# A diffusion block's cross attention: the context loaded with its inner dimensions exchanged and normalised in that form

## The reference

```python
q_c = _ln(x) @ W_qc + b_qc
kv_c = _ln(context) @ W_kvc + b_kvc          # context: 32 x 128 tokens x 128 channels
k_c, v_c = jnp.split(kv_c, 2, axis=-1)
...                                          # 16 heads of 8 channels
c_attn_w = jax.nn.softmax(jnp.einsum('bhqd,bhsd->bhqs', q_c, k_c) * scale, axis=-1)
c_attn_out = jnp.einsum('bhqs,bhsd->bhqd', c_attn_w, v_c)
...
x = x + c_attn_out @ W_cproj + b_cproj
```

## Time and profile before

| | |
|---|---|
| runs shown | median 561.09 us of 3 (560.26 to 562.99) |
| the profiled execution | 563.06 us, its span 561.2 us |
| granted TensorE clock, mean | 0.99 of full speed |
| setup, up to about | 30 us |
| attention rounds | about 30 to 300 us, 35 us a round |
| MLP and second layer | the rest |

### The profile page before, as it was taken

The page is one execution under the profiler, slowest core; times in us unless marked ns, Lnnn a source line. Parts: engine busy times, 40 slices in busy tenths (PEclk is TensorE's granted clock), DMA queues, the critical chain, the costliest instruction groups (busy, mean ns, idle before and its releaser), DMA issues.

```text
span 561.2 us, 16447 instructions
## 1 busy us (share of the span) xinstructions
PE 529.0 (94%) x6175; PEld 384.4 (68%) x6177; DVE 433.5 (77%) x1271; ACT 380.5 (68%) x889; POOL 276.2 (49%) x296
## 2 busy tenths in 40 slices
PE   6988999999999999999999989998999999999995
PEld 5745666666566665666676756665788788888885
DVE  4778889788989889888887667767586786786565
ACT  6537778587787886878787685555754864864862
POOL 5637849569498686888860413224124124124100
PEclk9989999899999999999999999999999999999998
DMA  4665635634254343543330001001011011010000
GB/s 133 153 181 137 179 100 151 139 94 106 61 137 120 79 125 81 132 117 100 82 79 4 2 23 36 1 20 37 3 39 56 23 35 56 23 38 14 20 20 19
DMA packets 52939, 41.47 MB, mean 74 GB/s; under 512 B 6369, under 2 KB 52226, under 8 KB 52866
## 3 DMA queue, kind: packets, MB, share of 16 engines
q1 hardware_dynamic: 50792, 36.72, 24.9%
q10 hardware_dynamic: 2074, 3.77, 2.4%
HBM read 12.16 MB, written 2.10 MB: 25 GB/s over the span
## 4 chain that ended last, share of the span: by engine, by line
PE 63%; DVE 15%; POOL 7%; DMA 5%; issue 4%; ACT 4%; SPq 2%; ACTq 0%; DVEq 0%; POOLq 0%
PE PS L958 31%; PE PS L1833 7%; PE PS L1799 5%; PE PS L1885 4%; DVE NM L1613 3%; PE PS L1897 3%; PE PS L994 2%; DMA Qs<-MT 2%; PE PS L1817 2%; PE PS L1855 2%; PE PS L1890 2%; SPq L1343 2%; DVE r_T L933 2%; DVE r_R L936 1%; PE PS L1877 1%
## 5 line engine op out<-in xcount | busy, mean ns | idle before, releaser
L1613 DVE TENSOR_REDUCE NM<-PS 128x4 f32<-128x512 f32 x256 | 163.3, 681 | 30.0 <-PE PS L1799 29.4
L1499 ACT ACTIVATE PR<-PS 128x512 f32<-128x512 f32 x256 | 139.7, 600 | 27.0 <-PE PS L1817 26.4
L1799 PEld LDWEIGHTS PS<-Ks,Qs 64*128 64x128 bf16 x1024 | 57.3, 94 | 53.8 <-DVE NM L1613 28.7
L1799 PE MATMUL PS<-Ks,Qs 64*128 64x128 bf16 x1024 | 83.4, 218 | 5.6 <-DVE NM L1613 3.8
L1817 PE MATMUL PS<-Qs,Ks 64*128 64x128 bf16 x1024 | 83.6, 218 | 3.9 <-DMA Qs<-MT 3.3
L1833 PE MATMUL PS<-PR,Va 128*32 128x128 f32 x2048 | 83.3, 281 | 0.0
L744 ACT ACTIVATE r_HID<-PS,ANC 128x128 f32<-128x128 f32 x224 | 62.4, 378 | 18.5 <-PE PS L958 18.5
L655 POOL TENSOR_TENSOR m_veps<-m_mv,m_eps 128x4 f32<-128x4 f32 x16 | 3.6, 225 | 129.7 <-DVE m_mv L820 129.7
L1833 PEld LDWEIGHTS PS<-PR,Va 128*32 128x32 f32 x2048 | 48.5, 110 | 20.2 <-ACT PR L1499 6.9
L1817 PEld LDWEIGHTS PS<-Qs,Ks 64*128 64x128 bf16 x1024 | 57.1, 94 | 7.5 <-DMA Qs<-MT 3.8
L958 PE MATMUL PS<-r_NXS,r_WNS 128*128 128x512 f32 x168 | 52.6, 421 | 0.0
(11 more groups left out here) (198 smaller groups left out, 1110.1 us busy)
## 6 DMA issues: line engine op xcount, KB each, us to landing
Qs<-Qp SPq DMA_DIRECT2D x96, 128.0 KB
Ks<-Kp SPq DMA_DIRECT2D x90, 128.0 KB
CTXG<-in_ctx SPq DMA_DIRECT2D x8, 256.0 KB, 3.9
r_CTX<-in_ctx SPq DMA_DIRECT2D x8, 256.0 KB, 2.9
r_CTXT<-in_ctxt SPq DMA_DIRECT2D x8, 256.0 KB, 3.3
out<-X SPq DMA_DIRECT2D x8, 256.0 KB, 2.3
X<-in_x SPq DMA_DIRECT2D x7, 256.0 KB, 4.5
W<-in_weights ACTq DMA_DIRECT2D x2, 855.0 KB
```

The costliest lines, as they stand in the source:

```text
L1499: nc.scalar.activation(PR[:, u, :], T_BANK[u % 2][:, :], ACT.Exp, scale=SCALE)\
L1613: nc.vector.tensor_reduce(out=NM[:, c.b // 2, c.second, u // 2, u % 2 * 4:u % 2 * 4 + 4, 0], in_=S_BANK[score_bank(c, u)[0]][:, :].rearran ...
L1799: last = nc.tensor.matmul(S_BANK[bank][:, j * P:(j + 1) * P], Qs[c.stack][rows, lo + j, cols], Ks[c.stack][rows, lo + j, cols], start=True ...
```

## The change

The context is also read from `in_ctxt`, an input that holds it with channels ahead of tokens (the second layer read it before already). A group now takes this way: `CTXG` is loaded and its statistics taken as before. Then three steps on SP, given by `spread_steps`: "rows store" waits for `rstd` and writes means and deviations, 512 numbers of 4 bytes each, to a scratch tensor `rows` in DRAM by two DMAs; "rows turned" loads the exchanged context to `XN[2]` or `XT[2]`, channels on partitions; "rows load" waits for the two stores and reads each row of 512 numbers back to all 128 partitions, the means over `CTXG`, the deviations to a new tile `ROWS`. POOL's norm then waits for these three loads and works in place on the exchanged tile; PE's `k` and `v` products read it. PE's transposes `xt_c` and ACT's copies are gone. The load of the next group's `CTXG` waits for the norm, as before.

```diff
+def spread_steps(t0, t1, t2, g):
+    return [(t0, "rows", "store", g, 0), (t1, "rows", "load", g, 0), (t2, "rows", "turned", g, 0)]
...
@@ regular_steps(i)
-            + stats_steps(19.2, 20.2, "ln_c", i) + norm_steps(23.0, "ln_c", i)
+            + stats_steps(19.2, 20.2, "ln_c", i) + spread_steps(26.0 if i == NG - 4 else 28.0, 29.0, 28.5, i) + norm_steps(29.5, "ln_c", i)
...
-            + fill_steps(14.0, "xt_c", i - 1, (1, 14.1))
...
@@ crossed_steps(i)
-    return (load_steps(1.0, g + 1) + stats_steps(5.2, 6.2, "ln_c", g + 1) + norm_steps(7.0, "ln_c", g + 1)
+    return (load_steps(1.0, g + 1) + stats_steps(4.9, 5.9, "ln_c", g + 1)
+            + spread_steps(8.05, 10.7, 9.0, g + 1) + norm_steps(14.1, "ln_c", g + 1)
...
-            + load_steps(12.0, g + 2) + stats_steps(21.2, 22.2, "ln_c", g + 2) + norm_steps(23.0, "ln_c", g + 2)
-            + fill_steps(0.2, "xt_c", g, (1, 0.3)) + fill_steps(2.0, "k0", i + 1, (0, 2.1), (1, 2.2))
+            + load_steps(12.0, g + 2) + stats_steps(19.2, 20.2, "ln_c", g + 2)
+            + spread_steps(22.0, 24.6, 25.1, g + 2) + norm_steps(27.0, "ln_c", g + 2)
+            + fill_steps(2.0, "k0", i + 1, (0, 2.1), (1, 2.2))
...
-            + fill_steps(16.0, "xt_c", g + 1, (1, 16.1)) + fill_steps(18.0, "k1", i + 1, (0, 18.1), (1, 18.2))
+            + fill_steps(18.0, "k1", i + 1, (0, 18.1), (1, 18.2))
...
+        rows = nc.dram_tensor("rows", [2, GB, P], F32).ap()
...
+        ROWS = sb("ROWS", [P, GT])
...
+        def context_turned(g):
+
+            return (XN[2], XT[2])[g % 2]
...
@@ SP
+                elif ev[:2] == ("rows", "store"):
+                    g = ev[2]
+                    sp.wait_ge(ln_rstd[2], g + 1)
+                    sp.dma_start(rows[0].rearrange("b p -> p b"), mv[:, 2, :, 0],
+                                 allow_slow_non_contiguous=True).then_inc(rows_stored, 16)
+                    sp.dma_start(rows[1].rearrange("b p -> p b"), rstd[:, 2, :],
+                                 allow_slow_non_contiguous=True).then_inc(rows_stored, 16)
+                elif ev[:2] == ("rows", "load"):
+                    g = ev[2]
+                    sp.wait_ge(rows_stored, 32 * (g + 1))
+                    for k, to in enumerate((CTXG[:, :, :].rearrange("p b h -> p (b h)"), ROWS[:, :])):
+                        row = rows[k:k + 1].rearrange("k b p -> k (b p)")
+                        sp.dma_start(to, row.to_broadcast([P, GT])).then_inc(rows_loaded, 16)
+                elif ev[:2] == ("rows", "turned"):
+                    g = ev[2]
+                    if g > 1:
+                        sp.wait_ge(*last_of_context(g - 2))
+                    sp.dma_start(context_turned(g)[:, :].rearrange("h (b p) -> h b p", b=GB),
+                                 ctxtin[bass.ds(g * GB, GB)].rearrange("b h p -> h b p")).then_inc(rows_loaded, 16)
...
@@ POOL
+                elif ev[:2] == ("norm", "ln_c"):
+                    if ev[3] == 0:
+                        g, turned = ev[2], context_turned(ev[2])[:, :]
+                        pool.wait_ge(rows_loaded, 48 * (g + 1))
+                        nc.gpsimd.tensor_tensor(turned, turned, CTXG[:, :, :].rearrange("p b h -> p (b h)"),
+                                                ALU.subtract).then_inc(ln_centred[2], 1)
+                        pool.wait_ge(ln_centred[2], g + 1)
+                        nc.gpsimd.tensor_tensor(turned, turned, ROWS[:, :], ALU.mult).then_inc(ln_done[2], 1)
...
@@ PE
+                        if name[0] == "k" and kind == CROSS:
+                            pe.wait_ge(ln_done[2], content(int(name[1]), g)[1] + 1)
```

More of the change, by code:

```diff
@@ L1193, in build_block @@
         ctx_loaded = sem("ctx_loaded")
+        rows_stored = sem("rows_stored")
+        rows_loaded = sem("rows_loaded")
         score_done = sem("score_done")
@@ L1241, in build_block @@
         OgT = [sb(f"OgT{k}", [P, GT]) for k in range(2)]
-        LN_KIND = {"ln_s": 0, "ln_x": 1, "ln_c": 2, "xt_s": 0, "xt_x": 1, "xt_c": 2}
+        ROWS = sb("ROWS", [P, GT])
+        LN_KIND = {"ln_s": 0, "ln_x": 1, "ln_c": 2, "xt_s": 0, "xt_x": 1}
         WEIGHT = {"q": ("q", "qc"), "k": ("k", "kc"), "v": ("v", "vc")}
@@ L1252, in turn_target @@
                 return XT[1]
-            return XT[0] if name == "xt_s" or isinstance(g, int) and g in (4, 6) else XT[2]
+            return XT[0]
         def source(name, it):
@@ L1259, in source, with last_of_context @@
                 return XT[mem]
-            return XT[1] if name[0] == "q" else XT[2 * mem]
+            return XT[1] if name[0] == "q" else context_turned(content(mem, it)[1])
+        def context_turned(g):
+            return (XN[2], XT[2])[g % 2]
+        def last_of_context(g):
+            mem = 0 if (CROSS, g) in HOLDS[0] else 1
+            return bank_filled[f"v{mem}"], HOLDS[mem].index((CROSS, g)) + 1
         def pair_of(c):
@@ L1397, in body @@
                     nc.gpsimd.memset(Ks[2][:, :, :].bitcast(F32), 0.0).then_inc(stack_init, 1)
+                elif ev[:2] == ("norm", "ln_c"):
[6 more added lines that the diff above has]
+                        nc.gpsimd.tensor_tensor(turned, turned, ROWS[:, :], ALU.mult).then_inc(ln_done[2], 1)
                 elif name == "norm" and not (ev[1] == "ln_x" and ev[2] in OF_DVE) and not (ev[1] == "ln_s" and ev[2] < 2):
                     g, k = ev[2], LN_KIND[ev[1]]
-                    x = CTXG[:, :, :] if k == 2 else X[:, bass.ds(g * GT, GT)].rearrange("p (b h) -> p b h", b=GB)
+                    x = X[:, bass.ds(g * GT, GT)].rearrange("p (b h) -> p b h", b=GB)
                     to = XN[k][:, :].rearrange("p (b h) -> p b h", b=GB)
@@ L1541, in body @@
                         last.then_inc(bank_read[name], 1)
-                elif name == "read" and ev[1] in ("xt_x", "xt_c"):
+                elif name == "read" and ev[1] == "xt_x":
                     name, g = ev[1:3]
@@ L1872, in body @@
                         return
-                    if name in ("xt_s", "xt_x", "xt_c"):
+                    if name in ("xt_s", "xt_x"):
                         k = LN_KIND[name]
```

4 lines of the change are left out of this document (2 added, 2 removed).

## The result

The changed kernel takes 662.31 us (median of 4 runs, 660.08 to 664.06) against 562.04 us for the kernel before beside it: ratio 1.177, 95% interval 1.171 to 1.182. The forecast was 576.0. The sign was right; the loss is 100 us where 15 were worked out. The profiled execution took 661.73 us, its span 659.8 us.

What follows compares the result with a forecast made beforehand. PE, 94% busy, paces the rounds, but delays of POOL or SP ahead of step 18 show almost in full. 4.3 + 2.9 + 3.7 + 2.0 + 2.0 = 14.9 us on 563.06 gives 578.0, or 576.0 as median; range 562.5 to 585.

Steps and rivals of the forecast that it cites:

- I take 2.3, since the bytes are few, and keep 3.9 as the bound.: Time in us from a store's issue to its landing in DRAM: 2.3 from `out`, bound 3.9 from the context's load.
- The third rival: Slow stores: landing 3.9 us or more instead of 2.3, total 585 and beyond with slower ones; chance 0.10.
- While SP waits for the stores to land, nothing urgent stands behind it: SP in C0 to C3: the row maxima of step 3 come some 9 us after those of step 27.
- The path that I wrote down for the regular rounds: C0 to C3: norm 1.0 to 1.75 us late, delaying `rstd`, splits, SP's moves and PE at step 18; +4.3 us.
- Row loads and norm: Per group: row loads land in 3.3 us, second issued 0.6 later; POOL's norm takes 2.2; whole chain 9.0 us.
- The crossed rounds, 2.9 + 3.7 + 2.0 + 2.0 = 10.6 us: Losses at C4 (end of round 4), round 5 up to step 18, second half of round 5, and round 6.
- The mechanism for C4's `k0`: Step 2 of round 5: PE waits in order for POOL's late norm of C4, about 3 us; term +2.9.
- where I charged 4.3: C0 to C3: norm ends 5.3 us too late in sum, less 1.0 PE may have had to spare.
- the first rival: Way through DRAM hidden in C0 to C3, only later rounds pay, 10.6 us at most: about 570; chance 0.22.
- What was to be seen: Profile signs: late norm of C0 to C3, PE's waits, SP waiting for `rows`, 32 fewer transposes.
- PE's waits for Q or K at step 18 of most rounds: PE should wait there for Q or K, longest in round 5, some 5 us.
- the stores' wait on SP is far from 2.3 us: One of three stated signs of being wrong: SP's wait for the stores' landing, taken as 2.3 us.

Runs made afterwards that it cites:

- the wide version: Changed kernel with mean and deviation in one store of 128 pieces of 32 bytes and one 512 KB row load per group: 598.4 us, ratio 1.060.

## Why the prediction was wrong

The direction and its reason, that PE's saved work counts for little and the way through DRAM for much, were right. The sum was wrong, by these steps.

1. **"I take 2.3, since the bytes are few, and keep 3.9 as the bound."** This step failed. The landing is 9.7 to 11.4 us after the second store's issue in the four regular rounds. The row of `out` was the wrong neighbour: its pieces are 512 bytes and this store's price is in its pieces. The bound was no bound either: it was the row of a load, and not even the slowest of 256 KB, since the page has 4.5 us for `X<-in_x`. The third rival had the cause, slow stores, at chance 0.10, but carried it only to 585 "and beyond", as a landing that is waited for.
2. **"While SP waits for the stores to land, nothing urgent stands behind it."** With a landing of 2.3 us that held; with 10.7 SP's wait pushed the row maxima of step 3 out by 6.8 us. And what I had not in the sum at all is that the stores delay what does not wait for them: 656 of 662 us in the version whose stores nobody reads, up to 51 us where they are added to the kernel before. The path that I wrote down for the regular rounds, norm too late, then splits, then SP's moves, did hold, with an overrun of 11.1 us for C2 where I had 1.0. But PE meets it first at the row maxima of step 11, which SP issues behind those moves; the waits for row maxima come to 40.2 us, those for K and Q to 2.6 and 1.9.
3. **Row loads and norm.** I took 3.3 us and 2.2 us. The loads land 4.3 to 6.5 us after the second one's issue in the regular rounds, and 8.1 for C5, so this term too was 30% to 100% too small there; the norm takes 180.25 to 182.86, 2.6.
4. **The crossed rounds, 2.9 + 3.7 + 2.0 + 2.0 = 10.6 us.** Without stores these rounds lose 309.94 - 214.28 - 72.0 = 23.7 us, the regular ones and round 4 together 1.6. The mechanism for C4's `k0` was the right one (I wrote about 3 us; 4.2 without stores, 5.4 with them). Two sizes were missing: issuing the row loads costs some 7.8 us even where no pass of POOL waits for them, and between its waits PE works at a granted clock of 0.87 (230 to 270 us) and 0.83 (270 to 310). In the regular rounds, where I charged 4.3, the gaps do hide a chain without stores; that much of the first rival was right.
5. **What was to be seen.** POOL's `veps` follows the norm without idling, there are 32 fewer transposes, SP waits for `rows`: so it came. PE's waits for Q or K at step 18 of most rounds did not: there are three. "I am wrong if … the stores' wait on SP is far from 2.3 us": 55.7 us in 7 waits, 8.0 on average.

Of the 100 us, then: some 75 are the stores' small pieces (662.3 less 587.5), 9 the wait for the row loads, 8 their issue and transfer, 6 the place and the passes of the norm; each is what taking it away in this order gave back, and the missing 2 are between the kernel before's times beside the two runs. What share of each is PE's clock is not settled: PE's busy time rises by 35.0 us in the changed kernel, 13.9 with stores alone and 0.6 without stores and rows, always with its waits, and no run held the clock up while keeping a wait.

## What to carry to other kernels

Price a transfer by its pieces and where they land, before its bytes: read how many contiguous runs the access pattern has at the DRAM end. If no row of the trace has such pieces, the bound upward is open, and the range has to say so. And ask of a slow transfer not only who waits for it, but what urgent small transfer is issued in the next ten microseconds on any queue. A busy share near nothing does not say that a transfer has landed, and waits that the profile gives to no instruction and no DMA are worth a look.

## What the runs showed of the hardware

- Stores to DRAM of 4 KB, in the regular rounds, from the end of the last issue: 1024 pieces of 4 bytes land after 9.2 to 10.7 us, 512 of 8 bytes after 3.4 to 4.5, 128 of 32 bytes after 1.1 to 2.2. The Trainium skill, page "DMA: Bandwidth & Descriptors", section Specifications, names read-modify-write below 512 bytes; all three lie below that, and their landings differ by a factor of four to ten.
- An 8 KB transfer issued behind 4-byte pieces took 10.6 us to land, with the DMA engines' busy share at 0.01 for six of them; behind pieces from another engine's queue one was late as well (PE waited 6.85 us). With 512 bytes between the pieces the cost to the kernel fell from 51 to 21 us.
- Among these runs, only with 4-byte pieces side by side do ACT and DVE wait, up to 5.8 us at a time in the changed kernel, with no instruction or DMA that the profile can name as the releaser.
- POOL's pass over 128 x 512 took 1.05 us with a small operand spread by its access pattern, 1.27 with a full second tile, and 1.54 where that tile is read with a step (first of two passes in the wide version):

```profile
153.78 1.54 POOL L1437 TENSOR_TENSOR XN<-XN,CTXG 128x512 f32<-128x512 f32 x1 [8.65 <-DMA CTXG<-rows]
```
